# First-batch column sums over four fp16 pair sums made on VectorE, in place of eight context tiles, with new instruction orders

## The reference

```
def fake_quant(x, s, z):
    q = clip(round(x / s + z), 0, 255)
    return (q - z) * s

x = x + matmul(fake_quant(layernorm(x), s1, z1), fake_quant(ctx, s2, z2))
y = layernorm(x)
weights, selected = top_k(einsum('bsd,ed->bse', y, gate_w), 2)
weights = softmax(weights)
low = einsum('bsd,erd->ebsr', y, lora_A)
x = x + einsum('bsd,od->bso', y, base_w) + base_b
      + 2.0 * einsum('ebsr,eor,bse->bso', low, lora_B, w_full)
```

## Time and profile before

| | |
|---|---|
| median of 3 runs | 175.3 us (175.26 to 175.56) |
| profiled execution | 175.75 us, of which the span is 173.1 us |
| PE busy | 163.6 us, 95% |
| DVE busy | 121.4 us, 70% |
| ACT busy | 72.8 us, 42% |
| POOL busy | 16.5 us, 10% |
| chain that ended last | PE 82%, DMA 8%, DVE 4% |
| mean granted clock of PE | 0.998 |

### The profile page before, as it was taken

The page is one execution under the profiler, slowest core; times in us unless marked ns, Lnnn a source line. Parts: engine busy times, 40 slices in busy tenths (PEclk is TensorE's granted clock), DMA queues, the critical chain, the costliest instruction groups (busy, mean ns, idle before and its releaser), DMA issues.

```text
span 173.1 us, 2404 instructions
## 1 busy us (share of the span) xinstructions
PE 163.6 (95%) x833; PEld 120.7 (70%) x833; DVE 121.4 (70%) x313; ACT 72.8 (42%) x128; POOL 16.5 (10%) x33
## 2 busy tenths in 40 slices
PE   5588999999999999999999999999999999999992
PEld 2133344689887888876887678976877698888881
DVE  0799799989999998899676748882772684135043
ACT  2279899891591259805510171231053110101150
POOL 3023004020040000000106010000003004000000
PEclk9999999999999999999999999999999999999999
DMA  4999999979866399800633969842007806630033
GB/s 117 397 399 417 410 410 407 272 153 336 336 121 123 82 357 413 182 2 0 121 61 58 187 123 164 260 110 76 2 0 134 229 4 107 135 121 0 0 121 121
DMA packets 13738, 30.58 MB, mean 177 GB/s; under 512 B 5408, under 2 KB 5408, under 8 KB 13728
## 3 DMA queue, kind: packets, MB, share of 16 engines
q1 hardware_dynamic: 11568, 23.11, 37.3%
q0 software_dynamic: 2016, 7.34, 22.8%
q10 hardware_dynamic: 144, 0.00, 0.0%
HBM read 22.05 MB, written 4.19 MB: 152 GB/s over the span
## 4 chain that ended last, share of the span: by engine, by line
PE 82%; DMA 8%; DVE 4%; SPq 2%; ACT 1%; issue 1%; ACTq 0%; DVEq 0%
PE ps_even L972 25%; PE ps_odd L972 25%; PE ps_att L918 10%; PE ps_g L954 6%; DMA ring<-in_ctx 6%; PE ps_t L899 4%; DMA x_sb<-in_x 2%; PE ps_g L957 2%; DVE x_sb L642 2%; ACT qc L387 1%; PE ps_odd L1015 1%; PE ps_even L1015 1%; PE ps_even L1013 1%; PE ps_even L1014 1%; PE ps_odd L1014 1%; PE ps_odd L1013 1%
## 5 line engine op out<-in xcount | busy, mean ns | idle before, releaser
L972 PE MATMUL ps_even<-w_hi,yt 128*128 128x512 f32 x128 | 37.8, 398 | 0.0
L972 PE MATMUL ps_odd<-w_hi,yt 128*128 128x512 f32 x128 | 36.5, 399 | 0.0
L972 PEld LDWEIGHTS ps_odd<-w_hi,yt 128*128 128x128 f32 x128 | 23.6, 188 | 5.2 <-issue 0.2
L972 PEld LDWEIGHTS ps_even<-w_hi,yt 128*128 128x128 f32 x128 | 23.6, 188 | 4.8
L918 PE MATMUL ps_att<-c,c1t 128*128 128x512 f16 x96 | 24.5, 380 | 0.2 <-DVE c L631 0.2
L443 ACT ACTIVATE yt<-ps_t 128x512 fp32r<-128x512 f32 x15 | 8.9, 593 | 30.0 <-PE ps_t L899 30.0
L972 PE MATMUL ps_even<-w_lo,yt 128*128 128x512 f32 x64 | 20.2, 392 | 0.0
L972 PE MATMUL ps_odd<-w_lo,yt 128*128 128x512 f32 x64 | 19.1, 393 | 0.0
L667 DVE TENSOR_TENSOR yt<-ps_t,yt 128x512 fp32r<-128x512 f32 x15 | 10.2, 683 | 11.5 <-ACT yt L443 11.5
L954 PE MATMUL ps_g<-ag,yt 128*128 128x272 f32 x64 | 16.6, 334 | 0.0
L376 ACT ACTIVATE ln_v<-mv,eps 128x1 f32<-128x1 f32 x16 | 4.7, 291 | 27.4 <-DVE mv L582 27.4
(11 more groups left out here) (104 smaller groups left out, 242.9 us busy)
## 6 DMA issues: line engine op xcount, KB each, us to landing
ring<-in_ctx SPq DMA_DIRECT2D x12, 512.0 KB, 7.1
w_raw<-in_w_t SPq DMA_DIRECT2D x8, 512.0 KB, 9.5
x_sb<-in_base_b POOLq DMA_DIRECT2D x8, 512.0 KB, 5.0
out_x<-x_sb SPq DMA_DIRECT2D x16, 256.0 KB, 2.3
x_sb<-in_x SPq DMA_DIRECT2D x7, 512.0 KB, 5.7
x_sb<-zfix POOLq DMA_DIRECT2D x6, 512.0 KB, 7.2
x_sb<-in_ctx SPq DMA_DIRECT2D x4, 512.0 KB, 5.4
ag_raw<-in_ag_t SPq DMA_DIRECT2D x1, 544.0 KB, 6.7
```

Of the source, the lines that this page charges most:

```text
L972: pe.matmul(ffn_bank[t % 2][h][:, :], rows_of(part, t, k), w[:, k, h * HALF:(h + 1) * HALF], start=start, stop=False)
```

## The change

1. DVE gets a new function, `pair_context(j)`: it adds context tiles 2j and 2j+1 of batch 0 into the new fp16 buffer `pairs`. The buffer of 4 x 1024 fp16 lies over `zfix`, `csum` and a new rest, which are written later.
2. `column_sums_first(j)` waits for a pair sum and multiplies ones with it: four tiles in place of eight, 8 matmuls in place of 16.
3. The written lists of all five engines are in another order through the whole program.

```diff
+        pairs_at = place[0]
         zfix = sb("zfix", [P, D], F32)
         csum = sb("csum", [P, D], F16)
+        sb("pairs_rest", [P, D], F16)
+        pairs = sb("pairs", [P, CT // 2, D], F16, at=pairs_at)
...
+            def pair_context(j):
+                dve.wait_ge(c2_ready, 2 * j + 2)
+                dve.tensor_tensor(pairs[:, j, :], c2[:, 2 * j, :], c2[:, 2 * j + 1, :], ALU.add).then_inc(pair_ready, 1)
...
-            def column_sums_first(k):
-                pe.wait_ge(c2_ready, k + 1)
+            def column_sums_first(j):
+                pe.wait_ge(pair_ready, j + 1)
                 for h in range(2):
-                    ins = pe.matmul(ps_even[h][:, :], ones[:, :], c2[:, k, h * HALF:(h + 1) * HALF],
-                                    start=(k == 0), stop=(k == CT - 1))
-                if k == CT - 1:
+                    ins = pe.matmul(ps_even[h][:, :], ones[:, :], pairs[:, j, h * HALF:(h + 1) * HALF],
+                                    start=(j == 0), stop=(j == CT // 2 - 1))
+                if j == CT // 2 - 1:
                     ins.then_inc(colsum_psum, 1)
...
             cut_context(6)
             cut_context(7)
-            x_constants(3)
+            pair_context(2)
+            pair_context(3)
             cut_x(2)
             add_attention(0)
+            x_constants(3)
             add_zfix(0)
```

More of the change, by code:

```diff
@@ L485, in _ @@
             first_guess(1, 1)
-            for k in range(3, 8):
+            for k in range(2, 8):
                 split_w_hi(k)
@@ L1071, in _ @@
-            for k in range(1, 5):
+            base_high(1, 0)
+            base_high(1, 1)
+            base_high(0, 6)
+            base_high(1, 2)
+            low_and_gate(1)
+            base_high(1, 3)
+            base_high(0, 7)
+            base_high(1, 4)
+            base_low(0, 0)
+            base_low(0, 1)
+            transpose_y(2, 0)
+            for k in range(2, 5):
+                base_low(0, k)
+            transpose_low(0)
+            for k in range(5, 7):
+                base_high(1, k)
@@ L1119, in _ @@
+            base(3, 7)
+            attention(5, 7)
             transpose_y(4, 1)
-            attention(5, 7)
-            transpose_low(3)
             base(4, 0)
             base(4, 1)
+            attention(6, 0)
             lora(3, 0)
-            for k in range(2, 5):
-                base(4, k)
-            low_and_gate(4)
-            lora(3, 1)
-            transpose_y(5, 0)
-            base(4, 5)
-            base(4, 6)
-            attention(6, 0)
+            lora(3, 1)
+            base(4, 2)
@@ L1133, in _ @@
+            transpose_y(5, 0)
+            base(4, 3)
+            base(4, 4)
+            low_and_gate(4)
+            attention(6, 1)
             transpose_y(5, 1)
[L1134 to L1135 removed]
+            for k in range(2, 6):
                 attention(6, k)
[L1137 to L1140 removed]
             base(5, 0)
             base(5, 1)
+            transpose_low(4)
@@ L1143, in _ @@
+            attention(6, 6)
+            attention(6, 7)
+            base(5, 2)
+            low_and_gate(5)
+            for k in range(3, 6):
+                base(5, k)
+            base(4, 5)
+            for k in range(0, 2):
+                base(4, k + 6)
+                attention(7, k)
+            base(5, 6)
             lora(4, 0)
-            base(5, 2)
-            base(5, 3)
+            lora(4, 1)
+            transpose_y(6, 0)
             transpose_low(5)
-            for k in range(0, 3):
+            base(5, 7)
@@ L1148, in _ @@
+            for k in range(2, 6):
                 attention(7, k)
-            lora(4, 1)
-            attention(7, 3)
-            base(5, 4)
-            transpose_y(6, 0)
-            base(5, 5)
-            base(5, 6)
-            attention(7, 4)
             transpose_y(6, 1)
-            for k in range(5, 8):
-                attention(7, k)
+            attention(7, 6)
+            attention(7, 7)
+            low_and_gate(6)
             base(6, 0)
             base(6, 1)
-            low_and_gate(6)
```

345 lines of the change are left out of this document (170 added, 175 removed).

## The result

The kernel after takes **180.99 us** (median of 4 runs, 179.81 to 181.92); the kernel before takes 175.28 us on the same chip. The ratio is 1.029, with a 95% interval of 1.024 to 1.035. The prediction was 176.8 us with a range of 175.4 to 178.5: the sign was right, but the size was 4 us short and outside the range.

A forecast was written before the change was run, and what follows sets the result against it. PE is full from 31.6 us on, so the end depends on when y, brought by DVE, lets it start. 175.3 us plus 1.2, 0.2 and 0.1 gives 176.8 us, range 175.4 to 178.5.

The forecast's parts named there:

- The first term: Ahead of PE's first transpose of y: four DVE pair sums, 2.40 us less 1.18 us idle cover; +1.2 us.
- context tile 7 was to land as before: At the start tile 7 stays SP's twelfth load, landing at about 19.7 us; its cut starts at 21.03 us.
- the 32.9: Sign of being right: y ended at 32.5 to 32.9 us.
- The second term: Behind the first transpose of y, new orders could gain nothing but might lose; +0.2 us, range 0 to 1.5.
- the three margins that were checked: DVE ahead of PE at b_lo by 0.4 us, at finished tile 0 by 0.5, at tile 1 79.2 against 80.8.
- the bound of 1.5 us: Upper end of the loss allowed where PE is full behind y, put at 0 to 1.5 us.
- The third term: At the end both last products stand together, the second finish starting 0.05 to 0.1 us later; +0.1 us.
- PE's clock falls in the gaps: Rival: between 9.9 and 15.1 us PE has little work, drops to 1.2 GHz; 177.3 to 180.1 us, chance 0.06.
- weight loads 0.43 us apart: Sign of being wrong: PE weight loads at this spacing, that of the lower clock, behind 12 us.
- Later waits: Rival: DVE brings b_lo or finished tile 0 late, PE stands 1 to 1.5 us; 178.0 us, chance 0.12.
- held by POOL: Rival: POOL's scaling holds up pair sums on DVE, 1.3 us more, none covered; 178.1 us, chance 0.06.
- PE waits of 1 us or more between 33 and 85 us: Sign of being wrong that would put the error into the second term.

The follow-up runs named there:

- e2: Changed kernel with 14 filler matmuls of ones on PE ahead of the attention of x tile 5; 181.69 us.
- h1: e1 with x tile 1 loaded ahead of context tile 0, as in the kernel before; 178.88 us, ratio 1.018.
- e5: Changed kernel with SP's first loads in the order of the kernel before; 180.42 us, ratio 1.023.
- e1: Changed kernel with POOL holding bias(3) and zfix(5) until the transposed x tile 5 has landed; 177.19 us, ratio 1.0063.
- f1: Changed kernel with zfix(5) issued first and only bias(3) held until the transposed x tile 5 has landed; 177.69 us, ratio 1.008.
- f4: Changed kernel with the hold of e1 and zfix(3) directly behind zfix(2) on POOL; 177.58 us, ratio 1.010.
- f3: Kernel before with only the first two pair sums, and column sums over these and context tiles 4 to 7; 176.37 us, ratio 1.003.
- h2: Kernel before with context tile 0 loaded ahead of x tile 1; 175.1 us, ratio 0.997.
- g2: Kernel before with 14 filler matmuls, then a PE wait for tile 4's bias, ahead of the attention of tile 5; 179.46 us, ratio 1.020.
- e6: Changed kernel with a second filler group and five more matmuls of ones on PE ahead of the first attention; 177.42 us, ratio 1.008.
- g1: Kernel before with a PE wait for tile 4's bias ahead of the attention of tile 5, no fillers; 180.97 us, ratio 1.026.

## Why the prediction was wrong

*The first term (+1.2), the pair sums ahead of y: about right in size, partly wrong in its make-up.* The sums cost what the row said, and the first two were hidden. The first transpose of y is later by 1.5 us (five traces against six, above). Of this, 0.9 us is the longer stretch behind tile 7: two sums, 1.20 us, less 0.28 us that the other order wins back, above all ahead of the first `add_zfix` (`add_attention` takes 1.32 us from start to start in place of 1.50). The other 0.6 us was put at nothing: context tile 7 was to land as before because it is still the twelfth load, at 1.26 us a load. But x tile 1 and context tile 0 had changed places too, and with them the rate from 5 to 8 us. So that 1.2 is close to 1.5 is in part luck. In after y ended at 33.29 us, past the 32.9 that was named as the sign of being right.

*The second term (+0.2), "the new orders behind it": this step failed.* In the trace of after the three margins that were checked held: PE does not wait between 33.4 and 97 us. (They were as thin as feared: in e2, h1 and e5 PE waited 1.1, 1.4 and 1.8 us at w_lo and b_lo.) The step took PE and VectorE as the only partners. It did not ask how long SP's transposing transfer of x tile 5 may take (8 us in both kernels) and what runs beside it now. The reordering of POOL's queue, which put bias(3) and zfix(5) ahead of bias(4), let them start 9.4 and 3.9 us earlier, beside that transfer. It took 11.0 us in place of 3.0. That nothing could be gained and a loss was possible was right, but the bound of 1.5 us was too low: the loss was 3.0 + 1.8 us by the trace, and 3.8 us by the medians of after and e1.

*The third term (+0.1), the end:* +0.02 us behind the last matmul. Right, and of no weight.

*The rivals.* "PE's clock falls in the gaps" had the mechanism, but at the start of the program, where it was free: the trace of after has weight loads 0.43 us apart from 12.31 us on, which the prediction had named as a sign of being wrong. But f1 without such a fall (granted clock 1.00 from 12 to 16 us) and f4 with it (0.57) both take 10.56 us from the cut of tile 7 (22.17 and 22.14) to y. The clock mattered at 100 us, behind a wait that no rival had. "Later waits" was right on b_lo for e2, h1 and e5, not for after. The pair sums were not held by POOL in after; in f3 one was, by 0.84 us. The sign that would have pointed at the second term, PE waits of 1 us or more between 33 and 85 us, did not come, since the wait is at 97 us.

*What is confirmed of the forecast.* Without the stall, the changed kernel is at ratios 1.0063 (e1), 1.008 (f1) and 1.010 (f4), which are +1.1 to +1.7 us on 175.3, and +1.7 to +1.9 us by the medians; the forecast was +1.5. No version was shown to beat the kernel before; h2 (0.997, interval to 1.000) comes nearest.

## What to carry to other kernels

Where the path is one full engine, look for each transfer that it will wait for: read the time from its issue to the first use, compare that with its longest landing and not its median, and list what any reordered queue now starts inside that interval, accumulating transfers above all. A wait of PE of some 3 us can have two prices, its length and the slower matmuls behind it (1.6 to 1.8 us in two traces here); fillers removed the second in the traces of e2 and g2, without a gain in time in e2, while a hold on the queue that crowds the transfer removed both (e1). A stretch that waits for loads is to be read from several executions before a cover of 1 us is counted.

## What was not expected of the hardware

The transposing transfer of 256 KB took 3.0 us alone (e1), 4.0 and 5.6 us beside one accumulating transfer of 512 KB, and 7.5 to 11.0 us beside two (six traces): more than the sum of the two single delays, which would give 6.6 us. From 92 to 98 us of after, the DMA engines are shown as full while they move little (busy time by stretch; the last two numbers are the DMA share and GB/s):

```profile
92.00:98.00 6.00, 5.07 (x23) 3.79 (x21) 5.03 (x18) 3.26 (x7) 0.00 (x0) 1.00 1.35 74
```

Loading a context tile ahead of the second x tile took a third off the rate of all transfers from 5 to 8 us (412 GB/s before, 272 after), for which no run here gives a cause. And the length of a wait did not by itself decide on PE's clock: PE kept 1.00 over 1.71 us of waiting behind fillers (g2) and over 2.77 us ahead of 9.43 us in before (1.00 from 9.4 to 12 us), while it had lost it after 2.77 us in e6, after 3.48 us in g1 and, early in after, behind 2.05 us without a weight load. The weight loads of after show the last case:

```profile
11.90 0.13 PEld L936 LDWEIGHTS ps_att<-c,c1t 128*128 128x128 f16 x2 [2.05 <-DVE c L640]
12.31 0.15 PEld L901 LDWEIGHTS ps_g<-ones 128*128 128x128 f16 x1 [0.28 <-issue]
12.74 0.15 PEld L901 LDWEIGHTS ps_g<-ones 128*128 128x128 f16 x1 [0.28 <-issue]
```
